# The product of the queries with the low part of the keys, contracted over 64 rows in two row tiles

## What is computed

```
x = x + attention(layer_norm(x))            # 8 heads of 64, 1024 tokens
q, k, v = xs @ Wq.T + bq, xs @ Wk.T + bk, xs @ Wv.T + bv
attn = softmax(q @ k.T / 8)                 # 1024 x 1024 for each head
out = (attn @ v) @ Wo.T + bo
t = t + ffn(layer_norm(t))                  # t: tokens of x; ffn = two small three-layer networks that
                                            # read a few channels and add to 33 of the 512
```

## Time and profile before

| | us |
|---|---|
| median of 3 runs (lowest, highest) | 2842.52 (2835.03, 2848.33) |
| the profiled execution | 2847.47 |
| its span, from the first to the last instruction | 2845.7 |
| PE busy in the span | 2572.5 (90%) |
| DVE busy | 1917.9 (67%) |
| ACT busy | 1736.0 (61%) |
| POOL busy | 900.3 (32%) |
| mean granted TensorE clock | 0.961 of full speed |

### The profile page before, as it was taken

How to read it: one execution, slowest core, us unless ns; L and a number is a source line. 1 busy time by engine, 2 the same in 40 slices (tenths; PEclk the granted TensorE clock), 3 DMA queues, 4 the chain that set the end, 5 groups by cost and what they waited for, 6 DMA issues and landing times. The chain is left out here.

```text
span 2845.7 us, 37765 instructions
## 1 busy us (share of the span) xinstructions
PE 2572.5 (90%) x13344; PEld 2093.9 (74%) x13344; DVE 1917.9 (67%) x3508; ACT 1736.0 (61%) x3048; POOL 900.3 (32%) x804
## 2 busy tenths in 40 slices
PE   4999898998899988999889989899898998999976
PEld 3788767887578766887768877688766887678864
DVE  4678656786477863877648776477765877567753
ACT  3677436774377734777347763477635775467732
POOL 0244303443044430443304433144421444124420
PEclk9999999999999998999999999999999999999997
DMA  6224103331113212222122231222402323032300
GB/s 234 60 72 121 74 17 85 78 104 74 51 52 88 93 74 61 60 71 93 75 61 71 71 112 44 63 69 74 152 1 72 78 63 145 1 89 71 93 30 30
DMA packets 79975, 215.54 MB, mean 76 GB/s; under 512 B 9968, under 2 KB 10256, under 8 KB 74000
## 3 DMA queue, kind: packets, MB, share of 16 engines
q1 hardware_dynamic: 79760, 212.77, 24.6%
HBM read 103.68 MB, written 25.17 MB: 45 GB/s over the span
## 5 line engine op out<-in xcount | busy, mean ns | idle before, releaser
L1036 POOL TENSOR_SCALAR PR_loop<-PR_loop,rinv_loop 128x1024 f32<-128x1024 f32 x448 | 503.7, 1124 | 1249.0 <-DVE rinv_loop L1004 1248.8
L1029 DVE TENSOR_TENSOR PL_loop<-pT_loop,PH_loop 128x512 fp32r<-128x512 f32 x896 | 576.0, 684 | 254.0 <-ACT PH_loop L984 252.4
L984 ACT ACTIVATE PH_loop<-pT_loop 128x512 fp32r<-128x512 f32 x896 | 487.2, 596 | 296.7 <-PE pT_loop L909 292.6
L999 DVE TENSOR_REDUCE nmax_loop<-pS_loop 128x1 f32<-128x1024 f32 x448 | 545.0, 1216 | 123.7 <-PE pS_loop L899 118.6
L954 ACT ACTIVATE PR_loop<-pS_loop,nmax_loop 128x1024 f32<-128x1024 f32 x448 | 501.2, 1119 | 24.8 <-DVE nmax_loop L999 22.5
L909 PE MATMUL pT_loop<-ident,PR_loop 128*128 128x128 f32 x3584 | 467.7, 273 | 18.1 <-POOL PR_loop L1036 18.1
L909 PEld LDWEIGHTS pT_loop<-ident,PR_loop 128*128 128x128 f32 x3584 | 415.2, 141 | 93.2 <-POOL PR_loop L1036 40.9
L898 PE MATMUL pS_loop<-KHL,QS 128*128 128x512 f32 x896 | 368.4, 411 | 58.5 <-issue 53.2
L930 PE MATMUL pO_loop<-PH_loop,VS 128*128 128x512 f32 x896 | 360.0, 402 | 21.5 <-DVE OT L1020 20.2
L931 PE MATMUL pO_loop<-PL_loop,VS 128*128 128x512 f32 x896 | 357.5, 399 | 0.0
L899 PE MATMUL pS_loop<-KHL,QS 128*128 128x512 f32 x896 | 356.8, 398 | 0.0
(11 more groups left out here) (284 smaller groups left out, 4065.5 us busy)
## 6 DMA issues: line engine op xcount, KB each, us to landing
KHL<-HL_loop SPq DMA_DIRECT2D x168, 256.0 KB, 3.6
WQ<-wqk_split SPq DMA_DIRECT2D x64, 512.0 KB, 5.8
QS<-HL_loop SPq DMA_DIRECT2D x168, 128.0 KB, 3.1
X<-in_x SPq DMA_DIRECT2D x32, 512.0 KB, 9.4
WO<-wo_split SPq DMA_DIRECT2D x16, 1024.0 KB, 6.8
X_loop<-in_x SPq DMA_DIRECT2D x28, 512.0 KB, 5.5
KHL<-wv_split SPq DMA_DIRECT2D x14, 1024.0 KB, 9.8
out<-X_loop SPq DMA_DIRECT2D x14, 1024.0 KB, 7.9
```

The source lines that it names most:

```text
L984: act.activation(PH[ck % 2][:, 4 * half:4 * half + 4, (g % 4) * P:(g % 4 + 1) * P], pT[half][:, :].rearrange("p (k n) -> p k n", k=4), ACT ...
L999: dve.tensor_reduce(nmax[:, g:g + 1], pS[g % 2][:, :], AX.X, ALU.max, negate=True)\
L1029: dve.tensor_tensor(PL[ck % 2][:, ks, qs], pT[half][:, :].rearrange("p (k n) -> p k n", k=4), f32(PH[ck % 2][:, ks, qs]), ALU.subtract).th ...
L1036: pool.tensor_scalar(PR[g % 2][:, :], PR[g % 2][:, :], rinv[:, g:g + 1], 1.0, ALU.mult, ALU.mult)\
```

## The change

The high passes stay as they are. The low pass no longer uses 128 rows. Only the 64 rows of q high meet k low, so the product of q low and k low is gone. k low of keys 0 to 511 lies in rows 0 to 63 of a new array `KL` (128 rows by 512), k low of keys 512 to 1023 in rows 64 to 127 of it. q high has to be in both halves of the rows: in rows 0 to 63 it is `QS`, in rows 64 to 127 a new array `QH`. A step still has four matmuls and four weight loads; two of them have 64 rows now, and they stand together at the end.

```diff
@@ attention, tensor: scores(g)
                 if t == 0 and h < 2:
-                    pe.wait_ge(S[f"f_kdup{h}"], 16)
+                    pe.wait_ge(S[f"f_kdup{h}"], 32)
                 if t == 0 and h >= 2:
-                    pe.wait_ge(S["a_qk"], 64 * NCH * (h - 1))
+                    pe.wait_ge(S["a_qk"], 96 * NCH * (h - 1))
                 if g >= 2:
                     pe.wait_ge(S["a_exp"], g - 1)
-                q = QS[h % 2][:, t * P:(t + 1) * P]
+                ts = slice(t * P, (t + 1) * P)
                 for n in range(NCH):
                     cs = slice(n * 512, (n + 1) * 512)
-                    pe.matmul(pS[g % 2][:, cs], q, KH[h % 2][:, cs], start=True, stop=False)
-                    mm = pe.matmul(pS[g % 2][:, cs], q, KL[h % 2][:, cs], start=False, stop=True)
+                    pe.matmul(pS[g % 2][:, cs], QS[h % 2][:, ts], KH[h % 2][:, cs], start=True, stop=False)
+                for n, q in enumerate((QS[h % 2][0:D, ts], QH[h % 2][D:P, ts])):
+                    mm = pe.matmul(pS[g % 2][:, n * 512:(n + 1) * 512], q, KL[h % 2][n * D:(n + 1) * D, :],
+                                   start=False, stop=True)
                 mm.then_inc(S["a_scores"], 1)
@@ attention, sync
                         sp.dma_start(f32(QS[h % 2][ps, cs]), f32(HL[0:D, half, :])).then_inc(S["a_qk"], 16)
-                        sp.dma_start(f32(T["KHL"][h % 2][ps, :, cs]), f32(HL[D:P, :, :])).then_inc(S["a_qk"], 16)
+                        sp.dma_start(f32(KH[h % 2][ps, cs]), f32(HL[D:P, 0, :])).then_inc(S["a_qk"], 16)
+                    sp.dma_start(f32(KL[h % 2][n * D:(n + 1) * D, :]), f32(HL[D:P, 1, :])).then_inc(S["a_qk"], 16)
+                    sp.dma_start(f32(QH[h % 2][D:P, cs]), f32(HL[0:D, 0, :])).then_inc(S["a_qk"], 16)
@@ network, sync
-                    sp.dma_start(f32(T["KHL"][h][0:D, :, :]), f32(T["KHL"][h][D:P, :, :]))\
-                      .then_inc(S[f"f_kdup{h}"], 16)
+                    sp.dma_start(f32(KH[h][0:D, :]), f32(KH[h][D:P, :])).then_inc(S[f"f_kdup{h}"], 16)
+                    sp.dma_start(f32(QH[h][D:P, :]), f32(QS[h][0:D, :])).then_inc(S[f"f_kdup{h}"], 16)
@@ split_qk
-    return dve.scalar_tensor_tensor(out=KLb[D:P, cs], in0=bank[D:P, :], scalar=bias[D:P, :],
+    return dve.scalar_tensor_tensor(out=KLb[n * D:(n + 1) * D, :], in0=bank[D:P, :], scalar=bias[D:P, :],
                                     in1=f32(KHb[D:P, cs]), op0=ALU.add, op1=ALU.subtract)
```

More of the change, by code:

```diff
@@ L103, in build @@
         VS = sb("VS", [P, ST, HEADS, 2 * D], F32R)
+        KH, KL, QH, OB, WV = [], [], [], [], []
+        for i in range(2):
+            at = nc.sbuf_base
+            KH.append(sb(f"KH{i}", [P, HW], F32R))
+            KL.append(sb(f"KL{i}", [P, 512], F32R))
+            at_q = nc.sbuf_base
+            QH.append(sb(f"QH{i}", [P, HW], F32R))
+            OB.append(nc.alloc_sbuf_tensor_at(f"OB{i}", [D, 512], F32, offset=at_q))
+            WV.append(nc.alloc_sbuf_tensor_at(f"WV{i}", [P, CT, C], F32R, offset=at))
         T = {
@@ L107, in build @@
             "QS": [sb(f"QS{i}", [P, HW], F32R) for i in range(2)],
-            "KHL": [sb(f"KHL{i}", [P, 2, HW], F32R) for i in range(2)],
+            "KH": KH, "KL": KL, "QH": QH, "OB": OB,
             "WQ": [sb(f"WQ{i}", [P, 2, CT, P], F32R) for i in range(2)],
@@ L112, in build @@
         }
-        T["WV"] = [z[:, :, :].rearrange("p a (b n) -> p (a b) n", n=C) for z in T["KHL"]]
+        T["WV"] = [z[:, :, :] for z in WV]
         dram = {
@@ L429, in network @@
         XH, XL, VS, QS, WQ = (T[k] for k in ("XH", "XL", "VS", "QS", "WQ"))
-        KH, KL = ([z[:, i, :] for z in T["KHL"]] for i in range(2))
+        KH, KL, QH = T["KH"], T["KL"], T["QH"]
         ident, b_qk, W0, W1H, W1L, W2S = (T[k] for k in ("ident", "b_qk", "W0", "W1H", "W1L", "W2S"))
@@ L825, in attention @@
         PR = [sb(f"PR{i}", [P, HW]) for i in range(2)]
-        OB = [sb(f"OB{i}", [D, 512]) for i in range(2)]
+        OB = T["OB"]
         QK = sb("QK", [P, 512])
@@ L882, in _ @@
                     sp.dma_start(T["X"][:, t, :], dram["x"][nxt, :, t, :]).then_inc(S["f_x"], 16)
-            sp.wait_ge(S["a_qk"], 64 * NCH * (HEADS - 2))
+            sp.wait_ge(S["a_qk"], 96 * NCH * (HEADS - 2))
         @block.tensor
@@ L991, in _ @@
                     if i > 0:
-                        act.wait_ge(S["a_qk"], 64 * i)
+                        act.wait_ge(S["a_qk"], 96 * i)
                     act.activation(HL[:, 0, :], QK[:, :], ACT.Copy).then_inc(S["a_proj_hi"], 1)
```

## The result

The changed kernel takes 2913.86 us (median of 4 runs, 2911.04 to 2920.18), the kernel before beside it 2838.78 us (4 runs). The ratio is 1.0264, 95% interval 1.0229 to 1.0298: 75 us slower. The forecast was 2962 us with a range of 2890 to 3030, from case B; what came is case A, which had been put at +72 us and a chance of 0.23.

The account below looks back on a forecast made before the run. TensorE was taken as the bound. At +0.28 us, 42 full steps add 11.8 us an image and 22 looser ones 6.2, half absorbed: 14.9 us, 119 us over eight images, giving 2962 us, range 2890 to 3030.

Parts of the forecast that it names:

- case B: Pair of 64-row matmuls: matmuls side by side, second weight load 0.11 us later; +0.28 us a step, 2962 us, chance 0.36.
- case A: Pair of 64-row matmuls: loads and matmuls side by side; +0.17 us a step, +72 us, 2915 us, chance 0.23.
- The bound: Attention, 2546 to 2690 us: TensorE busy for 144.00 of 144.00 us, so the time follows its list.
- the full stretch: The 42 of 64 attention steps where TensorE has no gap; they pay all, 42 x 0.28 = 11.8 us an image.
- The price of two changes: Each attention step goes from 128-row to 64-row matmuls and back: 0.20 us a change, 0.40 us a step.
- The pair: The two 64-row matmuls of a step: side by side they save 0.227 us, otherwise 0; the second load costs 0.11.
- The loose steps: 22 steps at the attention's ends: 6.2 us more work an image, half (3.1 us) absorbed by 8.3 us of waits.
- Costed at nothing: SyncE's six DMAs for a half head in place of four: no loss expected, 62 us at the very worst.
- Side D: Row changes in attention don't empty the array and the pair runs side by side: 76 us saved, 2766 us, chance 0.10.

Follow-up runs that it names:

- experiment 3: Kernel before with the low matmul of keys 512 to 1023 left out, three 128-row matmuls a step: 2752.06 us, ratio 0.9684.
- experiment 4: Kernel before with two more DMAs for each half head, into a tile that nobody reads: ratio 0.9994.
- experiment 1: Kernel before with both low matmuls of a step over rows 0 to 63, in the same row tile, after the high ones: 3027.57 us, ratio 1.0647.
- experiment 5: Changed kernel with the order high, low, high, low, so four changes of row count in a step: 3217.32 us, ratio 1.1339.
- experiment 8: Changed kernel with transposes directly behind the scores and made in 64-row tiles, 8 pairs in place of 8 full ones: 2885.55 us, ratio 1.0171.

## Why the prediction came out as it did

**The bound** was read rightly: TensorE's list in the full stretch. With a matmul less the time fell by 3%, with DMAs added it didn't move (experiments 3, 4). The way and the mechanism were right; 2914 us lies in the range because the range held nearly all of case A beside the case that was taken.

**The price of two changes**, 0.40 us a step from three places in the small networks, is the sum's main term; measured 0.405 and 0.8125 for four (experiments 1, 5). The trace of the kernel before, with 34-row matmuls in another stage, had priced it to 2%.

**The pair** is the term that was mis-sized. The prediction took B, "+0.28 us", because "the trace never shows two loads start closer than about 0.1 us". But all those loads are in the same rows, so they say nothing on loads in different rows. The measured loads start together (2632.62 both), and the step costs 0.181 us. 0.10 us x 42 steps x 8 images = 34 us, and some 10 us in the loose steps (14 measured, 25 forecast), are the 44 us by which the forecast of +119 was over the +75 measured. The Trainium skill's statement in "TensorE: Matmul & The Clock Gate", Part 3 (The mechanism), is that tiles in different row groups start about 4 ns apart. The trace agrees: 3 or 4 ns in all 512 pairs. It had been weighed against rows that could not contradict it, and should have had the larger chance.

**The changing of modes.** The Trainium skill, in "TensorEngine Tiling (Array Packing)", Key Properties, says that a change of tiling mode drains the engine. The trace agrees: about 0.09 us till the array is empty and 0.11 us of uncovered load for each change. The Trainium skill's "Up to 2×" for a dimension of 64 or less ("TensorEngine Tiling (Array Packing)", Theoretical Speedup) holds here for the pair alone, which takes 0.23 us where two full matmuls take 0.454. To gain by it the kernel would need a run of pairs: a pair saves 0.224 us and the two changes around it cost 0.405, so by these figures two pairs between two changes would just come out ahead. That is an estimate; no run has two such pairs.

**The loose steps** took up 57% of their price in the changed kernel and 34% of the dearer one (experiment 1; nearer 48% without what the clock cost there); the forecast was half. The 8.3 us of waits an image that it set this against leave out 17.0 us for VectorE in the loop, 2.4 an image.

**Costed at nothing**: confirmed by experiment 4 for the DMAs. Side D, the faster case, fell with the gaps at the 64-row loads. The clock stayed at its upper level in the full stretch (1.00 granted between 2594 and 2742 us), as expected, and the time at the lower level at the two ends of the attentions was the same as before.

## What to carry to other kernels

Before cutting a contraction to 64 rows, count the places where the row class changes, not the matmuls: here each costs 0.20 us, and a pair of 512 columns gives back 0.224 us. Group at least two pairs between two changes (by that sum; not run here), or bring neighbours that can be split (here the transposes) into the same class; then look at what waits when TensorE's list gets shorter, and at the granted clock behind those waits, since the two took the rest. A price for a change of class can be read off any stage of the old trace that has one, but rows of matmuls that all use the same array rows say nothing on two tiles.

## What was not expected of the hardware

- Two 64-row weight loads in different halves of the array start within 0.01 us of each other, and the second of the pair adds next to nothing to a step (0.224 of 0.227 us saved).
- 16 transposes of 64 rows and 64 columns in pairs take 0.58 us, 8 of 128 by 128 take 0.79.
- In experiment 8 a stretch of 3.4 us at the lower clock, behind a wait of TensorE of 1.6 us for GpSimd, costs 1.5 us.
- A matmul of 512 columns beside one of another row count in the same class is 0.235 us from its neighbour rather than 0.227; the 66-row ones of the networks show it as well.
